# First attention of a two-layer transformer: 64 unrolled slots, probabilities and queries turned by VectorE and DMA in place of TensorE

## The reference

```python
x = x + tanh(g_xattn[0]) * L0_xattn(layernorm(x), ctx, Wq, Wk, Wv, Wo, gq, gk)
x = x + tanh(g_ffn[0]) * L0_ffn(layernorm(x), ...)          # gate, up, down: packed 4-bit weights
x = x + tanh(g_xattn[1]) * L1_xattn(layernorm(x), ctx, ...)
x = x + tanh(g_ffn[1]) * L1_ffn(layernorm(x), ...)           # router, 8 experts, 2 of them a token

# L0_xattn: 16 heads of 128
q, k, v = rmsnorm(xn @ Wq, gq), rmsnorm(ctx @ Wk, gk), ctx @ Wv      # norms per head, eps 1e-5
out = softmax(q @ k.T / sqrt(128)) @ v @ Wo
```

## Time and profile before

| | us |
|---|---|
| profiled execution | 1293.64 |
| its span | 1291.9 |
| PE busy | 1238.0 (96%) |
| VectorE busy | 893.5 (69%) |
| ScalarE busy | 737.3 (57%) |
| GpSimd busy | 550.6 (43%) |

### The profile page before, as it was taken

The page is one execution under the profiler, slowest core; times in us unless marked ns, Lnnn a source line. Parts: engine busy times, 40 slices in busy tenths (PEclk is TensorE's granted clock), DMA queues, the critical chain, the costliest instruction groups (busy, mean ns, idle before and its releaser), DMA issues. The chain is left out here.

```text
span 1291.9 us, 23370 instructions
## 1 busy us (share of the span) xinstructions
PE 1238.0 (96%) x7907; PEld 1096.8 (85%) x7907; DVE 893.5 (69%) x2453; ACT 737.3 (57%) x2053; POOL 550.6 (43%) x542
## 2 busy tenths in 40 slices
PE   6899999999999989999999989999999998999998
PEld 4788888888888878888888889898898987888987
DVE  6678788887988767743433235757777688788857
ACT  4877777777777744332222237766656554546542
POOL 4565456545566433200000001766667778223430
PEclk9999999999999989999999989999999999999999
...
GB/s 268 10 1 1 9 1 1 1 9 0 0 0 1 65 41 2 64 331 293 65 0 1 1 18 17 152 120 123 115 107 142 124 126 251 119 46 101 131 100 174
DMA packets 85672, 101.09 MB, mean 78 GB/s; under 512 B 16985, under 2 KB 72802, under 8 KB 85186
## 3 DMA queue, kind: packets, MB, share of 16 engines
...
## 5 line engine op out<-in xcount | busy, mean ns | idle before, releaser
L98 PE MATMUL bank<-wvo_hi,pc_hi_a 128*128 128x256 f32 x512 | 148.8, 291 | 5.8 <-DVE pc_lo_a L1346 5.0
L1755 ACT ACTIVATE act_g_f<-bank 128x512 f32<-128x512 f32 x64 | 38.2, 598 | 191.1 <-PE bank L100 191.1
L100 PE MATMUL bank<-wvo_hi,pc_lo_a 128*128 128x256 f32 x512 | 143.8, 281 | 0.0
L99 PE MATMUL bank<-wvo_lo,pc_hi_a 128*128 128x256 f32 x512 | 143.7, 281 | 0.0
L1814 DVE TENSOR_TENSOR hid_f<-act_g_f,bank 128x512 f32<-128x512 f32 x64 | 44.0, 687 | 142.4 <-ACT act_g_f L1755 142.4
L883 ACT ACTIVATE probs_a<-bank,nbias_a,q_r_a 128x128 f32<-128x128 f32 x256 | 114.3, 472 | 23.6 <-DVE nbias_a L1001 23.4
L140 POOL TENSOR_TENSOR rstd<-mv,half 128x4 f32<-128x4 f32 x12 | 12.2, 1019 | 260.9 <-DVE mv L135 260.9
L1061 POOL TENSOR_TENSOR probs_a<-probs_a,rden_a 128x512 f32<-128x512 f32 x64 | 66.6, 1041 | 104.7 <-DVE rden_a L1007 104.7
L98 PEld LDWEIGHTS bank<-wvo_hi,pc_hi_a 128*128 128x128 f32 x512 | 97.4, 190 | 12.0 <-DVE pc_lo_a L1346 7.7
L1286 ACT ACTIVATE probs_a<-probs_a,nmin_a 128x128 f32<-128x128 f32 x256 | 99.6, 392 | 5.7 <-DVE nmin_a L1330 5.3
L98 PE MATMUL bank<-xt_hi_f,w_gu_hi_f 128*128 128x512 f32 (+1 forms) x256 | 101.2, 395 | 0.0
...
## 6 DMA issues: line engine op xcount, KB each, us to landing
...
staged<-blocks_a SPq DMA_DIRECT2D x32, 512.0 KB, 2.9
turned_a<-staged SPq DMA_DIRECT2D x128, 128.0 KB, 3.0
...
x_sb<-in_x SPq DMA_DIRECT2D x4, 512.0 KB, 9.9
```

Of the source, the lines that this page charges most:

```text
L98: nc.tensor.matmul(out, w[0], x[0], start=start, stop=False)
L99: nc.tensor.matmul(out, w[0], x[1], start=False, stop=False)
L100: return nc.tensor.matmul(out, w[1], x[0], start=False, stop=stop)
```

## The change

`attention` and its text of words are replaced by `first_order` and `first_attention`. The order is made by a function: slots v from -7 to 71, written out without a loop, with a fixed list of words for each, whose units lie apart (scores two units ahead, query projection seven ahead, C six behind; LAG is 8, H 16, U 64). The probabilities and the queries are no longer turned by TensorE. TQ: DVE turns blocks of 32 x 32 straight from the query bank (L815); TV: from the scaled probabilities (L846). For each pair of units, `swap` on SP writes the blocks to DRAM (L561) and reads them back in four parts (L567), for queries in odd slots and probabilities in even ones. Qc (ACT) copies the queries out of `q_turned`; Th and Tl both run on POOL (L909, L913). The sums of squares of two units' keys and queries stand in one tile of 128 x 16, and RT takes their root in one POOL instruction in every even slot (L889); eps is a 129th column of the squares. The fills K, Q, KT, X, CT, VT, VO take three banks in turn, C one. The packed feed-forward weights are loaded in parts, and CO waits for its part.

The diff, cut to its core:

```diff
-def quad_order(j):
...
-        CT1 Cl3 Qp3 CN0 S4 Sm4"""
...
+def first_order():
...
+    for v in range(-7, U + LAG):
+        s = v + 2 - LAG
+        if 0 <= v < U - H and v % H == 9:
+            words("X0 X1", v // H + 1)
+        unit(v + 2, "S")
+        unit(v + 6, "TQ", "Qq")
+        unit(v, "R", "Rp")
+        if v < U:
+            unit(v - 1, "TV")
+        unit(v + 3, "KT")
+        unit(v + 2, "Sm")
+        unit(v + 1, "EX")
+        unit(s, "C")
+        if v + 6 > 3:
+            unit(v + 6, "K")
+        if v + 5 > 3:
+            unit(v + 5, "Kr")
+        unit(v + 6, "Qr")
+        if v % 2 == 0:
+            unit(v + 4, "RT")
+        unit(v + 4, "KH")
+        words(lead.get(v, ""))
+        unit(s - 1, "W")
+        if 0 <= v < U - H:
+            words(norm.get(v % H, ""), v // H + 1)
+        if s >= 0 and (s % H, s // H) in ((15, s // H), (1, s // H)) and s > 1:
+            words("E0" if s % H == 15 else "E1", s // H - (s % H == 1))
+        unit(s, "Ch", "Cl")
+        if 0 <= s < U - H and s % H == 15:
+            words("CN0", s // H + 1)
+        unit(v + 3, "KTc", "Qc")
+        if v + 6 > 3:
+            unit(v + 6, "Kc", "Kq")
+        unit(s + 1, "Th", "Tl")
+        unit(v + 7, "Q")
+        if v == U - 1:
+            unit(v, "TV")
+        if s == U - 14:
+            words("LNF0")
+        for word in FEED.get(s, "").split():
+            order.append(("FF", 0, fed))
+            fed += 1
+    return order
...
+            def swap(p, made, source, via, sent, target, landed, free, taken):
+                s = p % 2
+                sp.wait_ge(sem(made), 2 * p + 2)
+                if p >= 2:
+                    sp.wait_ge(sem(f"{landed}{s}"), 64 * (p // 2))
+                sp.dma_start(via[s], source[:, s, :, :, :].rearrange("p j u x -> p (j u x)")).then_inc(sem(sent), 16)
+                if p >= 2:
+                    sp.wait_ge(sem(free), taken)
+                sp.wait_ge(sem(sent), 16 * (p + 1))
+                rows = via[s].rearrange("(i r) (j x) -> j r i x", i=4, j=4)
+                for j in range(4):
+                    sp.dma_start(target[32 * j:32 * j + 32, s, :, :, :].rearrange("p i u x -> p i (u x)"), rows[j]).then_inc(sem(f"{landed}{s}"), 16)
+
...
+            for v in range(-5, U + 1):
+                if v % 2:
+                    p = (v + 5) // 2
+                    if p < U // 2:
+                        swap(p, "q_blocks_made", q_blocks, staged[1], "q_blocks_sent", q_turned, "q_landed", "q_copied", 2 * p - 2)
+                elif v >= 2:
+                    p = (v - 2) // 2
+                    swap(p, "blocks_made", blocks, staged[0], "blocks_sent", turned, "landed", "pt_ready", 2 * p - 2)
...
+                if v in (53, 54, 55):
+                    sp.wait_ge(filled["Q"], U - QH)
+                    packed.load_words(sp, v - 53, 0)
...
+            def bank_free(step):
...
+                if at >= 3:
+                    old = ring[at - 3]
+                    pe.wait_ge(sem({"Q": "q_squared", "K": "k_copied", "KT": "kt_copied", "X": "x_split", "CT": "ct_split", "VT": "vt_copied",
+                                    "VO": "vo_split"}[old[0]]), count(*old))
+                return ring_bank[at % 3]
...
-                elif name == "QT":
-                    pe.wait_ge(sem("q_tok_copied"), nth(4, m, i))
...
-                        last = nc.tensor.transpose(bank[:, h * P:(h + 1) * P], q_tok[:, i % 2, h * P:(h + 1) * P], core.ident[:, :])
...
-                elif name == "T":
-                    pe.wait_ge(sem("probs_scaled"), nth(4, m, i))
-                    for h in range(QH):
-                        last = nc.tensor.transpose(t_bank[:, h * P:(h + 1) * P], probs[:, i % 2, h, :], core.ident[:, :])
-                    last.then_inc(sem("t_filled"), 1)
...
+                elif name == "C":
+                    if n % H == 0:
+                        pe.wait_ge(sem("cn_ready"), g + 1)
+                    pe.wait_ge(sem("pt_ready"), n + 1)
+                    if n:
+                        pe.wait_ge(sem("pc_ready"), n)
+                    three_pass(nc, c_bank[:, :], [v[:, b, :] for v in cn], [v[:, n % 2, :] for v in pt], True, True).then_inc(sem("c_filled"), 1)
...
-                elif name == "Qq":
-                    act.wait_ge(sem("q_tok_copied"), nth(4, m, i))
-                    nc.scalar.activation(q_sq[:, i % 2, :], q_tok[:, i % 2, :], ACT.Square).then_inc(sem("q_squared"), 1)
...
+                elif name == "Qc":
+                    act.wait_ge(sem(f"q_landed{n // 2 % 2}"), 64 * (n // 4 + 1))
...
+                    nc.scalar.activation(by_block(q[:, n % 2, :, :]), q_turned[:, n // 2 % 2, :, n % 2, :].rearrange("p i (h t) -> p i h t", h=QH),
                                          ACT.Copy).then_inc(sem("q_copied"), 1)
...
-                elif name == "Th":
-                    act.wait_ge(sem("t_filled"), nth(4, m, i))
-                    nc.scalar.activation(pt[0][:, :], t_bank[:, :], ACT.Copy).then_inc(sem("pt_hi_ready"), 1)
...
-                elif name == "Qv":
-                    if part == "start" and i >= 2:
-                        dve.wait_ge(filled["QT"], i - 1)
-                    dve.wait_ge(filled["Q"], nth(4, m, i))
-                    nc.vector.tensor_copy(q_tok[:, i % 2, :], bank[:, :]).then_inc(sem("q_tok_copied"), 1)
...
+                elif name == "TQ":
+                    dve.wait_ge(filled["Q"], n + 1)
+                    if n % 2 == 0 and p >= 2:
+                        dve.wait_ge(sem("q_blocks_sent"), 16 * (p - 1))
+                    nc.vector.transpose(q_blocks[:, p % 2, :, n % 2, :].rearrange("p j (h t) -> p h j t", h=QH),
+                                        bank[:, :].rearrange("p (h j s) -> p h j s", h=QH, j=4)).then_inc(sem("q_blocks_made"), 1)
...
-                elif name == "Qr":
-                    dve.wait_ge(sem("q_squared"), nth(4, m, i))
-                    nc.vector.tensor_reduce(q_ss[:, i, :], q_sq[:, i % 2, :].rearrange("p (h d) -> p h d", d=P), AX.X,
-                                            ALU.add).then_inc(sem("q_summed"), 1)
-                    dve.wait_ge(sem("q_summed"), nth(4, m, i))
-                    nc.vector.tensor_scalar(q_ss[:, i, :], q_ss[:, i, :], P * EPS, None, ALU.add).then_inc(sem("q_ss_ready"), 1)
...
+                elif name in ("Kr", "Qr"):
+                    kind, squares, low = (1, k_sq, "k") if name == "Kr" else (0, q_sq, "q")
...
+                    nc.vector.tensor_reduce(sums_of(kind, n), squares[:, n % 2, :, :], AX.X, ALU.add).then_inc(sem(f"{low}_summed"), 1)
...
-                elif name == "Tl":
-                    dve.wait_ge(sem("pt_hi_ready"), nth(4, m, i))
-                    nc.vector.tensor_tensor(pt[1][:, :], t_bank[:, :], f32(pt[0][:, :]), ALU.subtract).then_inc(sem("pt_ready"), 1)
+                    dve.wait_ge(sem("exp_done"), n + 1)
+                    nc.vector.reciprocal(rden[:, n % 2, :], den[:, n % 2, :]).then_inc(sem("rden_ready"), 1)
+                elif name == "TV":
+                    dve.wait_ge(sem("probs_scaled"), n + 1)
+                    if n % 2 == 0 and p >= 2:
+                        dve.wait_ge(sem("blocks_sent"), 16 * (p - 1))
+                    nc.vector.transpose(blocks[:, p % 2, :, n % 2, :].rearrange("p j (h t) -> p h j t", h=QH),
+                                        probs[:, n % 4, :, :].rearrange("p h (j s) -> p h j s", j=4)).then_inc(sem("blocks_made"), 1)
...
+                elif name == "RT":
+                    pool.wait_ge(sem("q_summed"), n + 2)
+                    pool.wait_ge(sem("k_summed"), n + 2)
+                    if p >= 4:
+                        pool.wait_ge(sem("exp_done"), n - 6)
+                    nc.gpsimd.tensor_tensor(roots[:, p % 4, :, :, :].rearrange("p k u h -> p (k u h)"), ss[:, p % 2, :, :, :].rearrange("p k u h -> p (k u h)"),
+                                            core.half[:, :], ALU.pow).then_inc(sem("roots_ready"), 1)
...
-                elif name == "Qp":
-                    pool.wait_ge(sem("q_ss_ready"), nth(4, m, i))
-                    nc.gpsimd.tensor_tensor(q_r[:, (j + 1) % 2, i, :], q_ss[:, i, :], core.half[:, 0:QH], ALU.pow).then_inc(sem("q_norm_ready"), 1)
...
+                elif name == "Th":
+                    pool.wait_ge(sem(f"landed{n // 2 % 2}"), 64 * (n // 4 + 1))
+                    if n >= 2:
+                        pool.wait_ge(sem("c_filled"), n - 1)
+                    nc.gpsimd.tensor_copy(pt[0][:, n % 2, :].rearrange("p (i x) -> p i x", i=4), turned[:, n // 2 % 2, :, n % 2, :]).then_inc(sem("pt_hi_ready"), 1)
+                elif name == "Tl":
+                    pool.wait_ge(sem("pt_hi_ready"), n + 1)
+                    hi, lo = (v[:, n % 2, :].rearrange("p (i x) -> p i x", i=4) for v in pt)
+                    nc.gpsimd.tensor_tensor(lo, turned[:, n // 2 % 2, :, n % 2, :], f32(hi), ALU.subtract).then_inc(sem("pt_ready"), 1)
...
             elif name == "CO":
```

(25 more changed lines are left out.)

752 lines of the change are left out of this document (261 added, 491 removed).

## The result

The changed kernel takes 1322.62 us (median of 4 runs, 1314.58 to 1324.48) against 1292.40 for the kernel before (4 runs beside it): a ratio of 1.0219, 95% interval 1.0175 to 1.0264. The profiled execution has a span of 1319.8 us, 27.9 more than before.

A forecast was written before the change was run, and what follows sets the result against it. TensorE was taken to bound the old kernel, a loop through VectorE, GpSimd and TensorE the new one. Feed-forward at 76.0 + 337.5 + 6.1 + 3.6 + 56.1 = 479.3, 1.3 us gained: 1291 us, range 1260 to 1322.

The forecast's parts named there:

- The loop: First attention: VectorE's turns, GpSimd's root to pt_lo, then TensorE's C to Q, closing at 13.50 us a pair of slots.
- the sum: Start of the feed-forward: 76.0 + 337.5 + 6.1 + 3.6 + 56.1 = 479.3 us, against 480.57 before.
- TensorE's waits in a pair: In the loop: some 1.8 us, 0.3 before the odd slot's KT and 1.5 before its C.
- added once: KT's bank late at slots 9, 25 and 41, 6.1 us; a norm's root in slots 20 and 36, 3.6 us.
- the opening: Fill of the first attention: slow first pairs, slots 0, 2, 4, 6 at 44.7, 55.7, 66.3, 76.0 us.
- the drain: From slot 56: GpSimd's Rp, pt_hi and pt_lo set 16 slots at 2.95 us; 56.1 us with the end.
- Rival C: TensorE's wait before the odd slot's C costs clock: every second pair, 13 x 2.6 = +34 us, 1325; chance 0.17.
- the prediction's own sign: In the first attention: a granted clock below 0.97 would show rival C right; the forecast expected 1.00.
- B: Rival: the loop doesn't close, TensorE sets 11.2 to 11.3 us a pair; 1236, half of it 1263; chance 0.14.
- D: Rival: turned blocks late (+60 us, 1350) or nbias waiting for Rp in the loop (+26, 1317); chance 0.13.
- The slow TENSOR_SCALAR: VectorE beside GpSimd's key scaling: 0.83 us against 500 ns, taken to agree with the shared-port lock rule.
- A STREAM_TRANSPOSE of a bank: VectorE's turn of queries in the loop: taken at 0.68 us; twice that would add 15 us over 25 pairs.

The follow-up runs named there:

- e2_c_late: The changed kernel with C moved behind K and W in TensorE's list of each slot: 1310.27 us, ratio 1.0143 to the kernel before.

## Why the prediction was wrong

**The loop: right.** 13.49 us against 13.50, with each link within 0.2 us: TQ to Kr 2.16 us (2.08 by the sum), the root 0.82 after Kr's start (0.75), `pt_lo` to C 1.35. TensorE's waits in a pair were put down as 0.3 us before KT and 1.5 before C; they are 0.75 and 1.2, 1.9 in all where 1.8 was said. The two runs with an added product show that it decides.

**What failed is the step "added once", with the opening and the drain, and the clock that the sum held at 1.00.** By the sum the feed-forward starts at 479.3, measured 512.18, 32.9 later. Three terms make it up. Slot 6 begins at 88.2 in place of 76.0: 12.2. From there to slot 56, forecast 337.5 + 6.1 + 3.6 = 347.2, measured 361.8 (the scores of slot 56 start at 450.0): 14.6. The drain, forecast 56.1, takes 62.2: 6.1.

By an estimate the 14.6 is nearly all clock. Pair by pair the trace has 24.1 us above 25 loops of 13.49, where the sum had 9.7. The pairs of slots 8, 24, 26 and 40, with the fills, take 9.8 more (17.67, 16.13, 13.87, 16.13); X was priced at 6.1 and CT at nothing. CT's six waits of 1.5 us come to 9.2, but most stand in place of the loop's own waits. The two pairs with the norm's root take 17.06 each, 7.1 more, priced at 3.6. Three pairs with nothing added, of slots 22, 38 and 46, take 15.01, 15.02 and 14.97, 4.5 more, priced at nothing. The first pair, 16.12, takes 2.6 more. Some pairs of each kind had the clock at half for a while. Its share, estimated from these pairs, is some 14 us: the 17.67 has 1.5 above the other 16.13, a root of 1.0 us alone would make 14.46 as the added product does (2.6 twice), and the 4.5 and the 2.6. Without it the fills' and the root's prices hold within 1 us together.

The 12.2 of the opening are explained in part. The scores of slot -2 start at 36.75, and from them to those of slot 6 it takes 51.4 us. With VT and VO out of the ring it takes 44.0, so some 5 to 7 us, with what it cost of the clock, are the ring's shift by VO, which the forecast had left out. What the rest of the opening is worth was not tried.

The drain was near for a wrong reason: two errors cancel. I gave every slot from 56 on 2.95 us, but the first four still have a root in each pair and a KH in each slot (GpSimd's lists), and take 25.8 us in place of 11.8:

```profile
451.27 0.48 PE L97 MATMUL bank<-pt_hi_a,cn_hi_a 128*128 128x512 f32 x1
...
477.05 0.48 PE L97 MATMUL bank<-pt_hi_a,cn_hi_a 128*128 128x512 f32 x1
```

What follows takes 35.1 us in place of 44.3; Rp ends with slot 63, and the last slots have only the two splits on GpSimd. The 1.2 us between slot 56's scores and its C make up the 62.2.

**Rival C comes nearest, with another count and price.** By the prediction's own sign, a granted clock below 0.97, it holds: 0.96 from 160 to 426 us. C wanted every second pair, 2.6 us each. Of the 16 pairs with nothing added 13 kept the clock and three lost it, 1.5 us each, behind the same waits (0.75 before KT, 1.2 before C). C's first product in slots 45 and 47, one pair apart, shows it:

```profile
376.81 0.50 PE L97 MATMUL bank<-pt_hi_a,cn_hi_a 128*128 128x512 f32 x1 [1.20 <-POOL pt_lo_a L913]
...
390.29 0.80 PE L97 MATMUL bank<-pt_hi_a,cn_hi_a 128*128 128x512 f32 x1 [1.20 <-POOL pt_lo_a L913]
```

Where one more microsecond stood in the pair, the norm or the added product, the clock fell more often. The scores made twice bring 12.0 us back, so this is a large part of the loss. That C's 1325 lies near the result is luck: it has 34 us on the loop, where the run has some 14 of clock there and the rest in the opening and the drain. What decides which of two equal pairs loses the clock, and whether it goes by the turns in the thin stretch or by the waits, stays open.

**Rivals B and D.** B is out: the loop closes. D too: C waited for GpSimd's work alone, and from 90 to 450 us GpSimd waited only for R and ahead of the root, so the swaps' landings of 3.3 and 2.7 us were hidden. The nbias of the loop took 0.16 us and waited for nothing. Where C is late (e2_c_late) it did take longer, and there the rule of the Trainium skill ("SBUF — State Buffer", "Who interferes with whom") agrees with the trace: nbias, two SBUF inputs, took 0.65 us and ended as GpSimd's `pt_lo` did (258.88 and 258.85). The slow TENSOR_SCALAR that I counted for the rule has one SBUF input, so it says nothing of a rule on two.

```profile
258.23 0.65 DVE L838 TENSOR_TENSOR nbias_a<-nmax_a,roots_a 128x4 f32<-128x4 f32 x1
```

```profile
257.56 1.29 POOL L913 TENSOR_TENSOR pt_lo_a<-turned_a,pt_hi_a 128x512 fp32r<-128x512 f32 x1
```

**A STREAM_TRANSPOSE of a bank** takes 0.715 us, near the 0.68 that I took from the one of SBUF; the link to its follower was 0.64 in place of 0.60.

```profile
L815 DVE STREAM_TRANSPOSE q_blocks_a<-bank 128x512 f32<-128x512 f32 x64 | 45.8, 715 | 65.1 <-PE bank L99 64.9
```
